# Four transformer blocks on one core: ScalarE's scalings and casts cut into pieces, and another order of the last attention steps

## The chip, the core and the metric

The kernel runs on one core of a Trainium2 chip and is written in Bass: each engine (TensorE, VectorE, ScalarE, GpSimd, and SyncE, which issues the DMAs) has its own program, and they meet in semaphores. The metric is the device time of one execution in microseconds. Before the change it is 1713.87 us, the median of three runs (1713.71 to 1713.95).

## The reference, cut to what matters

`x` has 16 tiles of 128 rows and 512 columns, and so has the context. Each layer adds its output to `x`, scaled with the tanh of a gate.

```python
x = x + tanh(g_xattn[0]) * L0_xattn(layernorm(x), ctx)   # retention
x = x + tanh(g_ffn[0])   * L0_ffn(layernorm(x))          # 8 experts, top 2, and a shared one
x = x + tanh(g_xattn[1]) * L1_xattn(layernorm(x), ctx)   # quantised attention, 16 heads, with cross attention
x = x + tanh(g_ffn[1])   * L1_ffn(layernorm(x))          # dense

# L1_xattn: the normalised input is scaled, clipped and rounded to fp8 for q, k, v; every head is
# normalised; softmax(q k^T) v over its own rows and over the context; the result is scaled by
# proj_smooth, rounded to fp8 and multiplied with wproj (4096 columns in, 512 out)
# L1_ffn:
logits = x @ W_gate.T
routing_weights, _ = top_k(logits, 2)
shared_out = relu(x @ W_up.T) @ W_down.T
expert_out = x @ W_expert
out = shared_out + sum(softmax(routing_weights)) * expert_out
```

## The kernel before

The 16 tiles are 4 chunks (`c`) of 4 tiles (`j`). One execution goes through the retention (`Retention`, `Values`), a block that sorts the rows to experts (`Sorting`), the experts (`Routed`), the shared expert with the quantisation for the next layer (`SharedAndQuantised`, `sh`), the attention, and the dense block (`Dense`, `de`). A barrier of all engines stands between the retention and `Sorting`. Each engine's program is an order written out by hand; an instruction waits for its semaphores, and all behind it on its engine wait too.

**Attention.** It has M = 64 steps: 4 quarters of heads times 16 tiles. `steps` (L2200) calls `step(i, ...)` for every `i` up to 66, since a tile is spread over steps: in step `i` TensorE does `keys_values` and `context_keys_values` of tile `i + 1`, `turn_probs` of `i - 1`, `output` (the projection) of `i - 3`, `turn` (transposes of the normalised heads, L2427) of `i`, `attend` (L2456) of `i - 1`, `scores` of `i` and `queries` of `i + 1`. ScalarE does `exps` of `i - 1` (L2577), `squares_b`, `rows_q`, `squares_a`, `probs_out`, `heads_out`, `values` (L2561), `rows_kv` (`x_kv`, L2522) and `scaled_out` (L2615). VectorE does `maxima` and `probabilities` of `i - 1`, the sum of squares (`sums_b`), the rounding of `y`, `normalise_b` (`t_hn`, L2680), `residual` and `normalise_a`; GpSimd does the power that gives 1 / deviation (`t_rs`) and splits the context.

From a score tile to the next tile's heads the chain runs: `maxima` (VectorE), `exps` (ScalarE), `squares_b` (ScalarE), the sum (VectorE), the power (GpSimd), `normalise_b` (VectorE), `turn` (TensorE).

**The last quantised chunk.** Each of its four slices `k` needs four scalings of 512 columns (`sh.scaled`, L1584; one for each of q, qx, k, v), then a rounding on VectorE in three operations (`sh.rounded`, L1686 to L1692), then a store by SyncE. `scaled` waits until the slice two before it is rounded, because there are two buffers. `LAST_ROWS = (1, 3, 4, 5)` names the steps at whose end ScalarE does all four scalings of a slice; VectorE rounds it at the end of the following step, ahead of that step's `maxima`, and SyncE stores it in between its loads.

**The projection's weight.** At the end of steps 2, 18, 34 and 50 ScalarE casts it (`wproj`, L2538) in two operations of 2048 columns.

**The way into the dense block.** In steps 63 to 66 the dense block's first work stands between the attention's: `de.turn` (transposes of normalised rows, L1863), `de.x_hi` and `de.x_lo` (the split of the transposed rows in a rounded part and a rest, L1870 and L1875), `de.up`, `de.relu`, `de.h_low`, `de.statistics`, `de.normalise`. On VectorE the methods `after_maxima` and `after_residual` place them by step. After that `Dense.tensor` starts with the gate logits of chunk 0, an expert matmul, and `turn_logits` (L1947), and goes on with `turn(3)` (transposes of chunk 3, again L1863).

**The end of the retention.** Each chunk's statistics (`tile_statistics`, L89 and L92) follow its four `x_res` rows. For chunks 0 to 2 GpSimd turns them into 1 / deviation (`row_factors`); for the last chunk ScalarE takes the root and VectorE the reciprocal, after the barrier. `low(2)` (L964), the rest of the split of chunk 2, stands after the barrier too.

## Time and profile before

| | before |
|---|---|
| median of 3 runs | 1713.87 us |
| profiled execution, its own time | 1714.87 us |
| its span | 1713.1 us |
| TensorE busy | 1630.4 us (95%) |
| ScalarE busy | 1102.9 us (64%) |
| VectorE busy | 1081.3 us (63%) |
| GpSimd busy | 480.9 us (28%) |
| DMA, share of 16 engines' span, main queue | 32.0% |
| mean granted TensorE clock | 0.989 |

The profile is one execution with one line for each instruction. In a timeline, equal neighbouring instructions are merged to a row; the brackets at its end give how long the engine was idle before it and what ended that. The durations of neighbouring matmuls and activations overlap, so the distance from start to start is what one costs in a row of them. TensorE's clock is granted at 2.4 GHz (1.00) or half of that.

### The profile page before, as it was taken

The numbers are of one execution on the slowest core, as the hardware profiler recorded it, in microseconds if no ns is written. First come the engines' busy times: TensorE is split into PE (matmuls) and PEld (weight loads), VectorE is DVE, ScalarE is ACT, GpSimd is POOL, SyncE is SP. The second block draws the span as 40 slices with busy tenths as digits, with TensorE's granted clock in tenths as the row PEclk, the third lists the DMA queues.
The fourth block names the chain that finished last, engine by engine and source line by source line (L and its number), as shares of the span: only waits on it lengthen the run. The fifth ranks groups of instructions, "written<-read, shape, count | busy, mean of one in ns | idle before, by whom it ended". The sixth has DMA issues, their size and how long they took to land.

```text
span 1713.1 us, 27138 instructions
## 1 busy us (share of the span) xinstructions
PE 1630.4 (95%) x9136; PEld 1337.7 (78%) x9136; DVE 1081.3 (63%) x2117; ACT 1102.9 (64%) x2974; POOL 480.9 (28%) x511
## 2 busy tenths in 40 slices
PE   6989779999998999999999999999999999998998
PEld 5888656666777778888788888788888788876887
DVE  6158854444876667777777776666666666786322
ACT  3454235543657888888888888878777878873100
POOL 1000122223424233433433433333443333420000
PEclk9999889999999999999999999999999999999999
DMA  6120649885663133364343353121151221100011
GB/s 242 49 80 34 266 138 315 299 287 168 235 237 125 50 127 145 113 265 164 113 152 130 127 225 117 57 86 55 56 233 56 69 79 55 56 25 1 25 37 37
DMA packets 74820, 219.67 MB, mean 128 GB/s; under 512 B 6288, under 2 KB 14480, under 8 KB 68304
## 3 DMA queue, kind: packets, MB, share of 16 engines
q1 hardware_dynamic: 69024, 199.56, 32.0%
q0 software_dynamic: 5680, 18.62, 3.5%
q8 instruction: 66, 1.08, 0.3%
q14 instruction: 50, 0.41, 0.1%
HBM read 157.60 MB, written 60.56 MB: 127 GB/s over the span
## 4 chain that ended last, share of the span: by engine, by line
PE 71%; ACT 5%; DVE 5%; DMA 4%; issue 1%; POOL 1%; another core or an unknown queue 0%; POOLq 0%; ACTq 0%; DVEq 0%
PE bank L2377 9%; PE bank L2378 9%; PE bank L97 7%; PE bank L98 7%; PE bank L99 7%; PE bank L2456 6%; PE bank L2438 6%; PE bank L2469 6%; PE bank L2427 5%; DMA s_rows<-x_rows,t_tok 4%; PE bank L2448 3%; PE bank L1349 3%; PE bank L1369 3%; ACT t_sc L2577 1%; ACT t_y L2615 1%
## 5 line engine op out<-in xcount | busy, mean ns | idle before, releaser
L2680 DVE TENSOR_TENSOR t_hn<-bank,t_rs 128x256 f32<-128x256 f32 (+1 forms) x256 | 130.8, 552 | 137.2 <-POOL t_rs L2342 70.4
L2377 PE MATMUL bank<-t_slot,t_x_q 128*128 128x512 f32 x512 | 205.5, 401 | 0.0
L2339 POOL TENSOR_SCALAR t_ve<-t_ss 128x4 f32<-128x4 f32 (+1 forms) x128 | 25.9, 202 | 628.6 <-DVE t_ss L2676 619.4
L2378 PE MATMUL bank<-t_slot,t_x_q 128*128 128x512 f32 x512 | 200.1, 391 | 0.0
L2577 ACT ACTIVATE t_sc<-bank,t_mx 128x128 f32<-128x128 f32 x512 | 183.9, 455 | 3.5 <-DVE t_mx L2700 3.5
L2342 POOL TENSOR_TENSOR t_rs<-t_ve,t_mhalf 128x4 f32<-128x4 f32 (+1 forms) x128 | 171.0, 1336 | 10.6
L2577 ACT ACTIVATION_READ_ACCUMULATOR t_sc<-bank,t_mx 128x1 f32 x512 | 151.6, 296 | 0.0
L2615 ACT ACTIVATE t_y<-bank,smooth 128x128 bf16<-128x128 f32 x512 | 139.2, 399 | 2.1 <-PE bank L2456 2.1
L2438 PEld LDWEIGHTS bank<-t_hT 128*128 128x128 f32 x1024 | 120.9, 192 | 15.8 <-ACT t_hT L2604 15.0
L2438 PE MATMUL bank<-t_hT 128*128 128x128 f32 x1024 | 131.4, 281 | 1.6 <-ACT t_hT L2604 1.6
L2377 PE MATMUL bank<-t_slot,t_x_kv 128*128 128x256 f32 x512 | 125.3, 283 | 2.1 <-DVE x_res L1647 1.4
L2378 PE MATMUL bank<-t_slot,t_x_kv 128*128 128x256 f32 x512 | 125.6, 283 | 0.0
L2707 DVE RECIPROCAL t_ri<-t_sm 128x4 f32<-128x4 f32 x128 | 22.7, 178 | 162.7 <-ACT t_sc L2577 162.7
L2469 PE MATMUL bank<-t_wp,t_cq 128*128 128x512 f16 x512 | 122.7, 383 | 1.4 <-DVE x_res L2723 1.4
L2456 PE MATMUL bank<-t_pT,t_vv 128*128 128x256 f32 x512 | 122.8, 383 | 0.0
L2377 PEld LDWEIGHTS bank<-t_slot,t_x_q 128*128 128x128 f32 x512 | 96.4, 188 | 18.7
L2378 PEld LDWEIGHTS bank<-t_slot,t_x_q 128*128 128x128 f32 x512 | 96.3, 188 | 18.6
L2427 PE MATMUL bank<-ident,t_hn 128*128 128x128 f32 x768 | 98.5, 275 | 12.1 <-DVE t_hn L2680 12.1
L2427 PEld LDWEIGHTS bank<-ident,t_hn 128*128 128x128 f32 x768 | 88.3, 142 | 27.4 <-DVE t_hn L2680 15.7
L2554 ACT ACTIVATE t_sqk<-bank 128x256 f32<-128x256 f32 x128 | 56.6, 457 | 80.3 <-PE bank L99 77.2
L2377 PEld LDWEIGHTS bank<-t_slot,t_x_kv 128*128 128x128 f32 x512 | 97.7, 191 | 5.1 <-issue 2.7
L2456 PEld LDWEIGHTS bank<-t_pT,t_vv 128*128 128x128 f32 x512 | 93.5, 193 | 10.4
(326 smaller groups left out, 4160.1 us busy)
## 6 DMA issues: line engine op xcount, KB each, us to landing
t_xh<-xq_scratch SPq DMA_DIRECT2D x64, 512.0 KB, 3.6
t_slot<-w_ready SPq DMA_DIRECT2D x16, 2048.0 KB, 8.4
t_cr<-in_ctxT_dram SPq DMA_DIRECT2D x64, 256.0 KB, 2.7
y_rows<-s_y SPq DMA_DIRECT2D x39, 256.0 KB
e_w<-in_w_units_dram SPq DMA_DIRECT2D x8, 1024.0 KB, 11.5
w_rows<-in_w_qkv_dram SPq DMA_DIRECT2D x8, 1024.0 KB, 7.2
w_ready<-w_hi SPq DMA_DIRECT2D x8, 1024.0 KB
w_ready<-w_lo SPq DMA_DIRECT2D x8, 1024.0 KB
```

What stands on the lines that cost most here:

```text
L97: nc.tensor.matmul(out, a_hi, b_hi, start=first, stop=False)
L98: nc.tensor.matmul(out, a_hi, b_lo, start=False, stop=False)
L2342: nc.gpsimd.tensor_tensor(rs[:, lo:hi], ve[:, lo:hi], mhalf[:, lo:hi], ALU.pow).then_inc(rs_in, 1)
L2377: nc.tensor.matmul(out, x_in[:, k, :], w[0][:, k, a:b], start=k == 0, stop=False)
L2378: last = nc.tensor.matmul(out, x_in[:, k, :], w[1][:, k, a:b], start=False, stop=k == KT - 1)
L2427: last = nc.tensor.transpose(b3[out][:, n, :], hn[:, h, :], env.ident[:])
L2438: last = nc.tensor.matmul(b3[4 + part][:, h, :], hT[:, (1 - part) * QH + h, :], hT[:, KH + (1 - part) * QG + h // 2, :], start=True, stop= ...
L2456: last = nc.tensor.matmul(bank[6 + part][:, g * 256:(g + 1) * 256], vv[par][:, (1 - part) * QG + g, :], pT[:, h:h + 2, :], start=True, sto ...
L2469: last = nc.tensor.matmul(bank[5][:], cq[par][:, h, :], wp[:, h, :], start=h == 0, stop=h == KH - 1)
L2577: last = nc.scalar.activation(sc[:, h, :], b3[4 + part][:, n, :], ACT.Exp, bias=mx[:, h:h + 1], accum_out=sm[:, h:h + 1])
L2615: nc.scalar.activation(y[:, part, ramp(h)], b3[6 + part][:, h, :], ACT.Copy, scale=env.smooth8[:, n:n + 1]).then_inc(y_in, 1)
L2680: nc.vector.tensor_tensor(hn[:, lo:hi, :], b3[bk][:, 0:hi - lo, :], rs[:, lo:hi].unsqueeze(2).broadcast_to([P, hi - lo, P]), ALU.mult).the ...
```

## The change

- `sh.scaled` takes the scalings one by one, and `ROW_PIECES` spreads the 16 of the last chunk over steps 1 to 6 (3, 1, 2, 3, 3 and 4 of them). Up to four places in a step take one: between the two squares of `squares_a`, after `heads_out`, after `values`, after `rows_kv`. VectorE's roundings and SyncE's stores stay where they were.
- `wproj` casts in four operations of 1024 columns: after `heads_out`, after `values`, after `rows_kv` and after `scaled_out` of steps 2, 18, 34 and 50.
- The loop of steps ends after step 62 on TensorE, ScalarE and VectorE. What was left stands in `last_steps`, written out for each engine, in another order. In `Dense.tensor` the first expert matmul stands ahead of the gate logits, and the second ahead of `turn_logits`.
- At the retention's end the statistics of three of the last chunk's tiles stand ahead of its last `x_res` row, GpSimd's `row_factors` does that chunk too, and `low(2)` follows ahead of the barrier. Root and reciprocal behind it are gone.

```diff
@@ Values.gpsimd, Values.vector, Sorting.vector
-        for c in range(C - 1):
+        for c in range(C):
             pool.wait_ge(self.final, (c + 1) * 2 * J)
             so.row_factors(pool, c)
...
+                if c == 3 and j == 2:
+                    dve.wait_ge(self.x_in, c * J + j + 1)
+                    for t in range(c * J, c * J + J - 1):
+                        v.bn_stats(env.st[:, t, :], env.x_res[:, t, :]).then_inc(self.final, 1)
             dve.wait_ge(self.x_in, c * J + J)
-            tile_statistics(nc, env, dve, self.final, c * 2 * J, range(c * J, c * J + J))
+            tile_statistics(nc, env, dve, self.final, c * 2 * J, range(c * J, c * J + J), J - 1 if c == C - 1 else 0)
+            if c == C - 1:
+                so.low(dve, 2)
...
-        v.tensor_scalar(self.var[:, 0:J], env.mv[:, last_rows, 1], LN_EPS, None, ALU.add).then_inc(self.var_in, 1)
-        dve.wait_ge(self.roots, 1)
-        v.reciprocal(env.rstd[:, last_rows], self.root[:, 0:J]).then_inc(self.rs_in, 1)
         self.normalise(dve, 3, range(J))
-        self.low(dve, 2)
@@ Dense.expert, Dense.tensor
         if n == 0:
             pe.wait_ge(self.wlo, self.n["expert"])
+        if n == 1:
             pe.wait_ge(self.rows_in, Q * B)
...
+        self.expert(pe, 0, 0)
         self.logits(pe, 0)
-        self.expert(pe, 0, 0)
+        self.expert(pe, 0, 1)
         self.turn_logits(pe, 0)
-        self.expert(pe, 0, 1)
         self.turn(pe, 3, range(2))
@@ attention
+    ROW_PIECES = {1: range(0, 3), 2: range(3, 4), 3: range(4, 6), 4: range(6, 9), 5: range(9, 12), 6: range(12, 16)}
...
+        def last_steps():          # TensorE
+            pe.wait_ge(n_in, M * 4 - 2)
+            de.turn(pe, 0, range(2))
+            turn_probs(M - 2)
+            output(M - 4, M % 2, M * 2 - 2, None)
+            de.turn(pe, 0, range(2, KT))
+            attend(M - 2, M % 2)
+            turn(M - 1)
+            de.turn(pe, 1, range(2))
+            scores(M - 1)
+            de.turn(pe, 1, range(2, KT))
+            de.up(pe, 0, 0)
+            de.up(pe, 0, 1)
+            turn_probs(M - 1)
+            output(M - 3, 1 - M % 2, M * 2, None)
+            attend(M - 1, 1 - M % 2)
+            de.up(pe, 0, 2)
+            output(M - 2, M % 2, M * 2, None)
+            de.up(pe, 0, 3)
+            de.turn(pe, 2, range(2))
+            output(M - 1, 1 - M % 2, M * 2, None)
+            de.turn(pe, 2, range(2, KT))
...
+        def rows_part(i, part):
+            pieces = ROW_PIECES.get(number(i), ())
+            if part < len(pieces):
+                k, v = divmod(pieces[part], 4)
+                sh.scaled(act, C - 1, k, (v,))
+
+        def wproj_part(i, part):
+            if isinstance(i, int) and i % B == 2 and i < M:
+                wproj(i // B, part)
...
             if has(i):
                 heads_out(i)
+            rows_part(i, 1)
+            wproj_part(i, 0)
             if has(i + 1):
                 values(i + 1, 1 - par)
+            rows_part(i, 2)
+            wproj_part(i, 1)
             if has(i + 2):
                 rows_kv(i + 2, par)
+            rows_part(i, 3)
+            wproj_part(i, 2)
             if has(i - 1):
                 scaled_out(i - 1, quarter)
...
-            if number(i) in LAST_ROWS:
-                sh.scaled(act, C - 1, LAST_ROWS.index(i))
-            if isinstance(i, int) and i % B == 2 and i < M:
-                wproj(i // B)
+            wproj_part(i, 3)
+
+        def last_steps():          # ScalarE
+            exps(M - 2)
+            squares_b(M - 1)
+            de.x_hi(act, 0, range(2))
+            probs_out(M - 2)
+            de.x_hi(act, 0, range(2, KT))
+            heads_out(M - 1)
+            de.x_hi(act, 1, range(2))
+            scaled_out(M - 2, None)
+            exps(M - 1)
+            de.relu(act, 0, 0)
+            de.x_hi(act, 1, range(2, KT))
+            de.relu(act, 0, 1)
+            probs_out(M - 1)
+            scaled_out(M - 1, None)
+            de.relu(act, 0, 2)
+            de.high(act, "expert", 0, KT)
+            de.relu(act, 0, 3)
...
+        def last_steps():          # VectorE
+            maxima(M - 2)
+            de.normalise(dve, 1, range(J))
+            probabilities(M - 2)
+            sums_b(M - 1)
+            de.x_lo(dve, 0, range(2))
+            rounded(M - 3, 1 - M % 2, 0)
+            normalise_b(M - 1)
+            de.x_lo(dve, 0, range(2, KT))
+            rounded(M - 3, 1 - M % 2, 1)
+            residual(M - 4, None)
+            de.x_lo(dve, 1, range(2))
+            maxima(M - 1)
+            de.statistics(dve, (10, 11))
+            de.aggregate(dve, 2)
+            probabilities(M - 1)
...
+            rounded(M - 2, M % 2, 1)
+            residual(M - 3, None)
+            de.statistics(dve, (12, 13))
+            de.normalise(dve, 2, range(J))
+            rounded(M - 1, 1 - M % 2, 0)
+            de.h_low(dve, 0, 2)
+            rounded(M - 1, 1 - M % 2, 1)
+            residual(M - 2, None)
+            de.low(dve, "expert", 0, KT)
+            de.h_low(dve, 0, 3)
+            de.x_lo(dve, 2, range(2))
+            residual(M - 1, None)
+            de.x_lo(dve, 2, range(2, KT))
+            de.statistics(dve, (14, 15))
+            de.aggregate(dve, 3)
```

The other lines of the diff drop what the old places held, and pass `end` and `done` to the helpers.

## Rows read from the trace of the kernel before

**Rows 1.** TensorE's waits by line: who was waited for, total us, times, longest us.

```profile
PE bank L2427 <- DVE t_hn L2680: 12.1, 9, 3.0
```

**Rows 2.** TensorE's timeline, `attend`: start us, us, engine, line, operation, idle before.

```profile
538.00 1.89 PE L2456 MATMUL bank<-t_pT,t_vv 128*128 128x256 f32 x8
556.08 3.62 PE L2456 MATMUL bank<-t_pT,t_vv 128*128 128x256 f32 x8
...
576.00 1.89 PE L2456 MATMUL bank<-t_pT,t_vv 128*128 128x256 f32 x8
...
628.20 1.89 PE L2456 MATMUL bank<-t_pT,t_vv 128*128 128x256 f32 x8
...
644.08 1.89 PE L2456 MATMUL bank<-t_pT,t_vv 128*128 128x256 f32 x8
...
818.60 1.89 PE L2456 MATMUL bank<-t_pT,t_vv 128*128 128x256 f32 x8
...
836.79 1.89 PE L2456 MATMUL bank<-t_pT,t_vv 128*128 128x256 f32 x8
```

**Rows 3.** ScalarE's timeline in steps 1 and 18, in the same columns.

```profile
535.17 0.38 ACT L2554 ACTIVATE t_sqk<-bank 128x256 f32<-128x256 f32 x1 [1.20 <-PE bank L99]
...
539.93 0.66 ACT L2561 ACTIVATE t_vv<-bank 128x256 f32<-128x256 f32 x2 [0.88 <-PE bank L2456]
...
543.42 2.98 ACT L1584 ACTIVATE z_y<-z_x3T,qb,qa 128x512 bf16<-128x512 f32 x4
546.24 0.42 ACT L2577 ACTIVATE t_sc<-bank,t_mx 128x128 f32<-128x128 f32 x1
...
820.53 0.66 ACT L2561 ACTIVATE t_vv<-bank 128x256 f32<-128x256 f32 x2 [0.24 <-PE bank L2456]
821.07 1.06 ACT L2522 ACTIVATE t_x_kv<-t_xh 128x1024 fp32r<-128x1024 f16 x1
822.02 2.17 ACT L2615 ACTIVATE t_y<-bank,smooth 128x128 bf16<-128x128 f32 x8
824.01 3.78 ACT L2538 ACTIVATE t_wp<-t_raw 128x2048 f16<-128x2048 f32 x2
827.61 0.43 ACT L2577 ACTIVATE t_sc<-bank,t_mx 128x128 f32<-128x128 f32 x1
```

**Rows 4.** VectorE's timeline in step 6: the last slice's rounding starts.

```profile
631.55 0.68 DVE L1686 TENSOR_SCALAR z_y<-z_y 128x2048 f16<-128x2048 bf16 x1
```

**Rows 5.** ScalarE's timeline, first `exps` after that rounding.

```profile
634.38 0.37 ACT L2577 ACTIVATE t_sc<-bank,t_mx 128x128 f32<-128x128 f32 x1 [0.59 <-DVE t_mx L2700]
```

**Rows 6.** TensorE's timeline on the way into the dense block.

```profile
1531.08 1.03 PE L1863 MATMUL bank<-ident,d_xn 128*128 128x128 f32 x8
...
1580.50 0.95 PE L1947 MATMUL bank<-fold,d_lgT 128*128 128x8 f32 x8
...
1584.18 1.04 PE L1863 MATMUL bank<-ident,d_xn 128*128 128x128 f32 x8
```

**Rows 7.** TensorE's waits from 1531 to 1585 us, by line.

```profile
PE bank L107 <- DVE d_xT_lo L1875: 2.8, 1, 2.8
PE bank L1863 <- DVE d_xT_lo L1875: 2.4, 2, 1.9
PE bank L1863 <- DVE d_xn L1852: 1.5, 1, 1.5
PE bank L2469 <- DVE x_res L2723: 1.4, 1, 1.4
```

**Rows 8.** Stretches: engines' busy us, mean granted clock, DMA share, GB/s.

```profile
1531.00:1563.00 32.00, 28.96 (x166) 22.10 (x163) 20.70 (x46) 19.84 (x57) 3.04 (x4) 1.00 0.00 1
1563.00:1578.00 15.00, 9.29 (x35) 5.84 (x34) 12.86 (x28) 3.12 (x6) 1.20 (x2) 0.77 0.00 1
```

**Rows 9.** VectorE's timeline, first `x_lo` of chunk 3.

```profile
1585.45 1.29 DVE L1875 TENSOR_TENSOR d_xT_lo<-bank,d_xT_hi 128x512 fp32r<-128x512 f32 x2 [0.31 <-ACT d_xT_hi L1870]
```

**Rows 10.** VectorE's timeline, last operation ahead of the retention's barrier.

```profile
189.46 0.38 DVE L92 BATCH_NORM_AGGREGATE mv<-st 128x2 f32<-128x6 f32 x4
```

More of the change, by code:

```diff
@@ L83, in cleared_semaphores, with tile_statistics @@
     nc.all_engine_barrier()
-def tile_statistics(nc, env, dve, stats, count, tiles):
-    for t in tiles:
+def tile_statistics(nc, env, dve, stats, count, tiles, done=0):
+    for t in tiles[done:]:
         nc.vector.bn_stats(env.st[:, t, :], env.x_res[:, t, :]).then_inc(stats, 1)
@@ L871, in __init__ @@
         self.tiles = [sb(f"tiles{i}", [P, 4 + E]) for i in range(3)]
-        self.var, self.root, self.dif, self.e1, self.s1 = (sb(n, [P, B]) for n in ("var", "root", "dif", "e1", "s1"))
+        self.dif, self.e1, self.s1 = (sb(n, [P, B]) for n in ("dif", "e1", "s1"))
         self.graw, self.posf, self.slot, self.row, self.ids = (
@@ L1582, in scaled @@
             act.wait_ge(self.q_in, n - 1)
-        for v in range(4):
+        for v in vs:
             nc.scalar.activation(self.y[n % 2][:, v * CW:(v + 1) * CW], source, ACT.Identity,
@@ L1889, in after_maxima @@
             self.aggregate(dve, 1)
-        if at == -1:
-            self.normalise(dve, 1, range(J))
     def after_residual(self, dve, at):
@@ L1905, in after_residual @@
             self.statistics(dve, (8, 9))
-        if at == -1:
-            self.x_lo(dve, 0, range(2, KT))
-            self.statistics(dve, (10, 11))
-            self.aggregate(dve, 2)
-            self.x_lo(dve, 1, range(2))
-        if at == 0:
-            self.statistics(dve, (12,))
-            self.h_low(dve, 0, 2)
-            self.h_low(dve, 0, 3)
-            self.normalise(dve, 2, range(J))
-        if at == 1:
-            self.statistics(dve, (13,))
-            self.x_lo(dve, 2, range(2))
-        if at == 2:
-            self.statistics(dve, (14,))
     def logits(self, pe, c):
@@ L2100, in vector @@
     def vector(self, dve):
-        self.statistics(dve, (15,))
-        self.aggregate(dve, 3)
-        self.x_lo(dve, 2, range(2, KT))
-        self.low(dve, "expert", 0, KT)
         self.normalise(dve, 3, range(J))
@@ L2202, in side, with steps @@
         return slice((1 - part) * QH, (1 - part) * QH + QH)
-    def steps(eng, step):
+    def steps(eng, step, end=M - 1):
         for i in range(B + FIRST):
@@ L2214, in steps @@
                     step(v * 2 + (first + 1), (FIRST + 1) % 2, quarter)
-            for i in range(first + 2 * loops, first + B):
+            for i in range(first + 2 * loops, min(first + B, end)):
                 step(i, i % 2, None)
@@ L2365, in gpsimd @@
         rstd(0, 0)
-        steps(pool, step)
+        steps(pool, step, M + FIRST)
         de.rstd(pool, 2)
@@ L2513, in tensor @@
         steps(pe, step)
+        last_steps()
         de.tensor(pe)
@@ L2530, in rows_q, with wproj @@
                                  ).then_inc(xq_in, 1)
-        def wproj(quarter):
-            if quarter:
+        def wproj(quarter, part):
+            i, a = divmod(part, 2)
+            if quarter and part == 0:
                 act.wait_ge(pj_ps, quarter * B)
-            act.wait_ge(wraw_in, quarter * 16 + 16)
+            if part == 0:
+                act.wait_ge(wraw_in, quarter * 16 + 16)
             raw = slots32[homes[quarter][SPARE]]
-            for i in range(2):
-                nc.scalar.activation(wp[:, 4 * i:4 * i + 4, :], raw[:, i], ACT.Copy).then_inc(wp_in, 1)
+            last = nc.scalar.activation(wp[:, 4 * i + 2 * a:4 * i + 2 * a + 2, :], raw[:, i, 2 * a:2 * a + 2, :], ACT.Copy)
+            if a:
+                last.then_inc(wp_in, 1)
+        def rows_part(i, part):
[6 more added lines that the diff above has]
+                wproj(i // B, part)
         def squares_a(m):
@@ L2734, in step @@
                 probabilities(i - 1)
-            if number(i) == M:
-                de.x_lo(dve, 1, range(2, KT))
-                de.h_low(dve, 0, 0)
             if has(i) and later(i, 1):
@@ L2741, in step @@
                 rounded(i - 2, par, 0)
-            if number(i) == M - 1:
-                de.x_lo(dve, 0, range(2))
-            if number(i) == M:
-                de.h_low(dve, 0, 1)
             if number(i) == M - 3:
@@ L2773, in step @@
                 sh.rounded(dve, C - 1, LAST_ROWS.index(i - 1))
+        def last_steps():
[14 more added lines that the diff above has]
+            probabilities(M - 1)
+            de.h_low(dve, 0, 0)
+            de.x_lo(dve, 1, range(2, KT))
+            rounded(M - 2, M % 2, 0)
+            de.h_low(dve, 0, 1)
+            rounded(M - 2, M % 2, 1)
[13 more added lines that the diff above has]
+            de.aggregate(dve, 3)
         sh.normalise(dve, C - 1)
```

48 lines of the change are left out of this document (7 added, 41 removed).

## The prediction

> **What bounds the kernel now.** I read the page first: TensorE is busy 95% of the span, and two thirds of the span (504 to 1570 us) are 64 attention steps. Then the waits of TensorE by line: the largest sum inside the attention is the transposes of the normalised heads, which stood 12.1 us for VectorE's `t_hn` [rows 1]. Then TensorE's timeline, one row per step (the row of `attend`): it shows where steps are longer than usual. A usual step is 15.88 us, from 628.20 to 644.08, with no idle time: there TensorE alone sets the pace. Between attend 0 (538.00) and attend 5 (628.20) stand 90.20 us. Four usual steps and the step into attend 1, which has no `output` yet (15.87 less the 1.73 from the start of `output` to the next group, so 14.14), make 77.6 us: 12.6 us are lost [rows 2]. From attend 17 to attend 18 stand 18.19 us, so 2.3 are lost, and the same after the casts of quarters 2 and 3: 7.0 us in three places. The rest of the middle has nothing to give. Last I read the way from attention to the dense block: from 1531.08, the first `de.turn`, to 1584.18, the first `turn` of chunk 3, stand 53.10 us [rows 6], with 8.1 us of waits in four rows [rows 7] and a mean granted clock of 0.77 in 1563 to 1578 [rows 8].
>
> **Why pieces of ScalarE work cost time.** ScalarE goes from `values` through `rows_kv` and `scaled_out` to the next `exps` without a pause; its last pause before that is 0.24 us ahead of `values`, or 0.88 in a step in which TensorE has been held. Two casts of 2048 columns moved `exps` from 824.01 to 827.61, by 3.60 us; four scalings of 512 columns moved it from 543.42 to 546.24, by 2.82 [rows 3]. `exps` leads to the squares, VectorE's sum, GpSimd's power and VectorE's `t_hn`. The delays of 3.60 and 2.82 lost 2.3 and 1.5 us a step (the latter from attend 2 at 576.00 to attend 5 at 628.20, three steps of 17.40 [rows 2]), so this chain has 1.3 us of slack: a step loses the delay of its `exps` less 1.3. That rule carries the first sum.
>
> **The last quantised chunk.** Its 16 scalings ran as four blocks; they become 3, 1, 2, 3, 3 and 4 pieces in steps 1 to 6. One piece takes 2.82/4 = 0.71 us. The first of a step goes between the two squares, where ScalarE stood 1.2 us for TensorE [rows 3]: free. The second goes ahead of `values` and fills the 0.24 or 0.88 us. The others count in full.
> - Step 1: one piece counts, delay 0.71, and the power chain has 1.73 us less slack in the step without `output`, so it loses 0.71 - (1.3 - 1.73) = 1.1. Now it loses 3.9 there, with the wait of 3.0 [rows 1], and TensorE falls to half speed: attend 1 took 3.62 us where 1.89 is usual [rows 2]. A stall of 1.1 should not bring that on; the saved 2 us lie in step 2's present loss of 4.1.
> - Step 2: one free piece and all four parts of the weight cast, three of them in full (below): delay 2.9, loss 1.6.
> - Step 3: nothing. Step 4: 2 x 0.71 - 0.24 = 1.2. VectorE's rounding of a finished slice stands ahead of the maxima: from its start (631.55) to `exps` (634.38) stand 2.83 us [rows 4, 5]; by that way too the delay is 1.2. Step 5 gives 1.3. Both are at the edge of the slack: loss 0 to 0.1 each.
> - Step 6 is the new stall. Its last piece stands behind `rows_kv`, and the rounding of that slice, in VectorE's program ahead of the maxima, waits for it. From `values` on, with a piece ahead of it (0.47 late): pair of casts 0.54, piece 0.71, `x_kv` 0.95, piece 0.9 to its end makes 3.6; rounding to `exps` 2.83. So `exps` starts 6.4 us after the usual start of `values` instead of 3.48 [rows 3]: delay 2.9, loss 1.6. SyncE's store of the slice waits for the rounding too, 2.1 us later than now, and behind it in SyncE's queue stand the KV weights, `t_cr` and `t_xh` of tile 9. By my sum `t_xh` comes 0.1 us before it is wanted; I price it at 0, with 0.5 as the other end.
> Together 1.1 + 1.6 + 0 + 0.1 + 1.6 = 4.4 us lost against 12.6: **8.2 us gained** (5 to 10).
>
> **The weight casts of quarters 1 to 3.** Two of 2048 columns become four of 1024. `x_kv`, also 1024 columns, holds ScalarE from 821.07 to 822.02, 0.95 us [rows 3]. All four stand between `heads_out` and `exps` of the same step, so the delay is 4 x 0.95 - 0.24 = 3.56 against 3.60: nothing is gained, 0.1 us in all. The waits that they put ahead of `values`, `x_kv` and `y` (0.7, 1.7 and 2.6 us) are hidden: TensorE wants `x_kv` 3.7 us after it is now ready. The page Perfetto Trace Analysis of the Trainium skill (§ Optimizing Scalar/DVE Operations) says that breaking up instructions helps where an unsaturated ScalarE causes bubbles elsewhere. It would have these three stalls shrink; rows 3 show no pause for the pieces to fall into. That is the second rival.
>
> **The last steps.** On TensorE the same items stand in a new order. Their durations without stalls, from start to start of the 24 groups in the timeline from 1531.08 to 1584.18 [rows 6]: a pair of turns 0.87 (six), a turn of probabilities 0.87 (two), `output` 1.73 (four), `attend` 1.73 (two), head turns 1.31, scores 1.80, `up` 2.72 (four), experts 2.72 (two), gate logits 1.82, their turn 0.81. Sum 39.4. So 13.7 us are lost now: 8.1 in the waits, 15 x (1 - 0.77) = 3.4 from half speed [rows 7, 8], the rest in a small wait and in restarts.
> I walked the new order with these durations and those of ScalarE and VectorE. Squares now come ahead of the copies of `xT`, the sum follows the probabilities at once, and x_lo(0) is done at 1534.6, as TensorE wants it: the wait of 1.9 goes. Scores 63 follow the head turns with only one pair of turns between, but need all copies of the heads (3.05 us after the head turns start, as in usual steps): a new wait of 0.9. `turn_probs` 63 comes 1.4 us after its probabilities. Both last `output`s find their rounded input, because `up` 2 and 3 stand between them. `normalise` 2 is done at 1555 for a turn at 1560, x_lo(2) at 1564.9, while the expert matmul (now ahead of the logits) covers until 1566. So turn 3 starts at 1531.1 + 39.4 + 0.9 = 1571.4 instead of 1584.2: 12.8 us.
> What is late next: the turn of the logits moved behind the second expert, so VectorE's gate weights and its x_lo(3) come closer to the turns that need them. x_lo(3) starts 4.95 us after the turn of the logits (1580.50 to 1585.45 [rows 6, 9]), its first slice is done 0.65 later; TensorE has 0.81 + 0.87 + 2.72 = 4.4 us of work. A new wait of about 1.0. Left: **11.8 us gained** (7 to 12.8).
>
> **The front.** Statistics of three tiles go under the last `output`, the root goes to GpSimd, and `low(2)` moves ahead of the barrier. VectorE reached the barrier at 189.84 [rows 10]; it is to be done with the statistics 1.8 us earlier and then does four `low`s of 0.62, so it is there 0.65 later. `normalise` 3 still starts where it did. GpSimd's constants, for which the turn of the logits waits, start 0.65 later too; about 0.4 of it is made up behind, where TensorE now waits for x_lo(3) and no longer will: **0.2 us lost** (0.4 gained to 0.7 lost). The block behind (routing on VectorE) is unchanged.
>
> **Sum.** 8.2 + 0.1 + 11.8 - 0.2 = 19.9 us. The profiled execution took 1714.87 us, 1.0 above the median of the runs, and its span is 1713.1; I take the gain off both alike: 1695.0 for a profiled execution and 1713.87 - 19.9 = **1694.0 us** for the median. The forecast's own range, from the bounds of its parts, is 1691 to 1698.
>
> **Rivals.**
> - The pieces work everywhere, also in quarters 1 to 3: the three losses of 2.3 us go. For it: the edit is the same as in steps 1 to 5, where it helps. Against it: all four parts stand in one step without a pause. 1694.0 - 6.9 = 1687.1. 8%.
> - The last steps give half: a wait that my walk gets wrong by a microsecond (the scores, x_lo 3, the last `output`) brings the half-speed clock back, as two waits of 1.5 and 1.4 us do now. 1694.0 + 5.9 = 1700. 13%.
> - The first edit does not do what it says: the pieces only move the same ScalarE work and the delays of `exps` stay, with late slices behind SyncE's queue. 1713.9 - 11.7 = 1702. 6%.
> - Slower: TensorE stays at 1.2 GHz through the whole transition. Half speed was granted right when it had idled at 551 and again after 1563, and the new order has short waits of 0.9 and 1.0. At half speed the 39.4 us of work take 39.4 more, so 1694.0 + 39.4 = 1733.4; it makes the kernel slower from 20 us of work at half speed on. Against it: the granted clock was 1.00 from 1531 to 1563, past a wait of 1.9 [rows 7, 8]. 2%.
> The forecast has 69%, 2% is left for what I don't see. A difference of 0.2% (3.4 us) is about what a measurement of this kernel can tell from none. Range: the forecast, and to 1701 for the second rival, which holds 82%: 1689 to 1701. Faster 0.95, same 0.02, slower 0.03.
>
> **What would show it.** Right: attend 1 to 5 at full speed, steps 4 and 5 near 15.9 us, a stall of 1.6 in the head turns of step 7, where none is now; steps 18, 34 and 50 still with 2.3; in the last steps one wait of 0.9 ahead of scores and one of 1.0 at turn 3. Wrong: steps 18, 34 and 50 at 15.9 (rival one), a granted clock below 1 after 1530 (rivals two and four), `exps` as late in steps 2 to 5 as now (rival three), or a wait for `t_xh` near tile 9.

## The result, and the profile after

The changed kernel takes 1693.2 us, the median of four runs (1690.65 to 1694.76), beside 1713.91 us for the kernel before, now of four runs: a ratio of 0.9872, 95% interval 0.9853 to 0.9892. The two medians lie 20.7 us apart. Two later series gave 0.9888 (0.9865 to 0.9911) and 0.9897 (0.9874 to 0.9920). As gains the three ratios are 21.9, 19.2 and 17.6 us. In the later series single executions of the kernel before took 1707 to 1719 us, so each ratio is known to 0.2% and no better. 1694.0 was forecast.

The profiled execution took 1690.65 us (span 1688.9). The spans of the two profiles differ by 24.2 us, more than the medians. Part of it isn't the change's: at attend 0 the second profile is already 4.17 us ahead, and nearly all of that comes from the routed and the shared experts, whose code is the same (last section).

The page's first lines, busy time and the granted clock in 40 slices of the span:

```profile
PE 1625.2 (96%) x9136; PEld 1337.6 (79%) x9136; DVE 1081.9 (64%) x2115; ACT 1104.6 (65%) x2981; POOL 482.0 (29%) x513
...
PEclk9999979999999999999999999999999999999999
```

TensorE's timeline of the changed kernel, the row of `attend` (L2435), with the head turns (L2406) ahead of two of them; columns as in [rows 2]:

```profile
533.83 1.89 PE L2435 MATMUL bank<-t_pT,t_vv 128*128 128x256 f32 x8
549.14 1.89 PE L2435 MATMUL bank<-t_pT,t_vv 128*128 128x256 f32 x8
566.60 1.89 PE L2435 MATMUL bank<-t_pT,t_vv 128*128 128x256 f32 x8
...
630.50 1.25 PE L2406 MATMUL bank<-ident,t_hn 128*128 128x128 f32 x8 [1.04 <-DVE t_hn L2686]
631.59 1.89 PE L2435 MATMUL bank<-t_pT,t_vv 128*128 128x256 f32 x8
...
647.59 1.89 PE L2435 MATMUL bank<-t_pT,t_vv 128*128 128x256 f32 x8
...
806.26 1.89 PE L2435 MATMUL bank<-t_pT,t_vv 128*128 128x256 f32 x8
...
823.22 1.25 PE L2406 MATMUL bank<-ident,t_hn 128*128 128x128 f32 x8 [1.31 <-DVE t_hn L2686]
824.31 1.89 PE L2435 MATMUL bank<-t_pT,t_vv 128*128 128x256 f32 x8
```

These answer [rows 2]. Each `attend` takes 1.89 us: the one of 3.62 is gone. From attend 0 to 7 stand 113.76 us, where 121.93 stood before: **8.17 us gained**. The step into attend 18 takes 18.04 us where 18.19 stood, so the stall of quarter 1 is still there, with its wait of 1.31 for `t_hn`; those of quarters 2 and 3 are alike (18.04 and 18.05). From attend 7 to 61: **0.3 us gained**. TensorE's waits for `t_hn` over the whole profile (total, times, longest), beside [rows 1]:

```profile
PE bank L2406 <- DVE t_hn L2686: 7.7, 7, 1.3
```

ScalarE's timeline in steps 6 and 18, which answers [rows 3 and 5]:

```profile
618.77 0.83 ACT L1582 ACTIVATE z_y<-z_x3T,qb,qa 128x512 bf16<-128x512 f32 x1
619.47 2.19 ACT L2613 ACTIVATE t_y<-bank,smooth 128x128 bf16<-128x128 f32 x8
622.47 0.37 ACT L2575 ACTIVATE t_sc<-bank,t_mx 128x128 f32<-128x128 f32 x1 [0.81 <-DVE t_mx L2706]
...
807.83 1.06 ACT L2522 ACTIVATE t_wp<-t_raw 128x1024 f16<-128x1024 f32 x1
...
814.15 1.15 ACT L2522 ACTIVATE t_wp<-t_raw 128x1024 f16<-128x1024 f32 x1
815.10 0.46 ACT L2575 ACTIVATE t_sc<-bank,t_mx 128x128 f32<-128x128 f32 x1
```

In step 18 the four parts stand between 807.83 and 815.10, where ScalarE has no pause left, and `exps` starts 8.84 us after attend 17 (806.26). Before it was 9.01; in a usual step it is 5.42. The delay is still 3.42. In step 6 `exps` waits for the maxima behind the last slice's rounding.

The way into the dense block, in TensorE's timeline (L1861 `de.turn`, L2417 scores, L1928 `turn_logits`), then two stretches of it with TensorE's busy time, granted clock, DMA share and GB/s; these answer [rows 6, 7 and 8]:

```profile
1518.42 1.03 PE L1861 MATMUL bank<-ident,d_xn 128*128 128x128 f32 x8
...
1527.55 2.05 PE L2417 MATMUL bank<-t_hT 128*128 128x128 f32 x16 [0.70 <-ACT t_hT L2602]
...
1558.15 0.95 PE L1928 MATMUL bank<-fold,d_lgT 128*128 128x8 f32 x8
1558.96 1.15 PE L1861 MATMUL bank<-ident,d_xn 128*128 128x128 f32 x8
1563.52 1.16 PE L1861 MATMUL bank<-ident,d_xn 128*128 128x128 f32 x8 [0.68 <-DVE d_xT_lo L1873]
```

```profile
1518.00:1550.00 32.00, 31.30 (x184) 1.00 0.00 1
1550.00:1565.00 15.00, 14.32 (x80) 1.00 0.01 1
```

From the first `de.turn` to turn 3 stand 40.54 us instead of 53.10. The clock is 1.00 in both stretches, and only the two forecast waits are left, 0.70 and 0.68. From attend 61 to the last `turn_logits` 90.70 us instead of 102.24: **11.54 us gained**. With the 4.17 ahead of attend 0 that makes 24.18.

### The profile page after: what moved, and what is told of

It reads as the page before. It is cut to its first block, busy times and chain, and to the rows that moved or that the text cites. A ratio compares the mean times of both kernels' runs of the same rounds, so it can differ in the third digit from the quotient of the medians.

```text
span 1688.9 us, 27156 instructions
## 1 busy us (share of the span) xinstructions
PE 1625.2 (96%) x9136; PEld 1337.6 (79%) x9136; DVE 1081.9 (64%) x2115; ACT 1104.6 (65%) x2981; POOL 482.0 (29%) x513
## 4 chain that ended last, share of the span: by engine, by line
PE 76%; ACT 4%; DVE 3%; DMA 3%; POOL 1%; issue 1%; ACTq 0%; POOLq 0%; DVEq 0%
PE bank L2356 10%; PE bank L2357 10%; PE bank L97 7%; PE bank L98 7%; PE bank L99 7%; PE bank L2417 7%; PE bank L2435 6%; PE bank L2448 6%; PE bank L2406 5%; PE bank L1347 3%; PE bank L1367 3%; PE bank L2427 3%; DMA s_rows<-x_rows,t_tok 2%; PE bank L1327 1%; ACT t_sc L2575 1%
## 5 line engine op out<-in xcount | busy, mean ns | idle before, releaser
L2417 PEld LDWEIGHTS bank<-t_hT 128*128 128x128 f32 x1024 | 120.2, 191 | 16.8 <-ACT t_hT L2602 16.2
L2417 PE MATMUL bank<-t_hT 128*128 128x128 f32 x1024 | 131.0, 281 | 2.3 <-ACT t_hT L2602 2.3
L2435 PE MATMUL bank<-t_pT,t_vv 128*128 128x256 f32 x512 | 121.1, 379 | 0.0
L2406 PEld LDWEIGHTS bank<-ident,t_hn 128*128 128x128 f32 x768 | 87.6, 141 | 22.7 <-DVE t_hn L2686 10.7
L2406 PE MATMUL bank<-ident,t_hn 128*128 128x128 f32 x768 | 97.3, 274 | 7.7 <-DVE t_hn L2686 7.7
L97 PE MATMUL bank<-t_slot,t_c_hi 128*128 128x512 f32 x256 | 100.4, 392 | 0.0
```

The costliest lines, as they stand in the source:

```text
L97: nc.tensor.matmul(out, a_hi, b_hi, start=first, stop=False)
L2406: last = nc.tensor.transpose(b3[out][:, n, :], hn[:, h, :], env.ident[:])
L2417: last = nc.tensor.matmul(b3[4 + part][:, h, :], hT[:, (1 - part) * QH + h, :], hT[:, KH + (1 - part) * QG + h // 2, :], start=True, stop= ...
L2435: last = nc.tensor.matmul(bank[6 + part][:, g * 256:(g + 1) * 256], vv[par][:, (1 - part) * QG + g, :], pT[:, h:h + 2, :], start=True, sto ...
```

## The experiments

**Each part alone.** Four kernels, each the kernel before with one part of the change. The interval after each ratio to the kernel before is the 95% one.

*Only the pieces of the last chunk:*

```diff
+    ROW_PIECES = {1: range(0, 3), 2: range(3, 4), 3: range(4, 6), 4: range(6, 9), 5: range(9, 12), 6: range(12, 16)}
...
-            if number(i) in LAST_ROWS:
-                sh.scaled(act, C - 1, LAST_ROWS.index(i))
             if isinstance(i, int) and i % B == 2 and i < M:
                 wproj(i // B)
```

> The kernel before with the last quantised chunk in pieces, and nothing else (the weight casts stay two of 2048 columns at the end of steps 2, 18, 34, 50). Slack theory: a step loses the delay of its exps beyond 1.3 us. Step 1 loses 1.1, step 2 has a delay of 3.6 and loses 2.3, step 6 loses 1.6, against 12.6 now: 7.5 us gained between attend 0 and attend 7, nothing elsewhere, about 1706.4. If the pieces only moved the same work (the third rival of the prediction), 0 to 2 us would be gained and exps in steps 2 to 5 would be as late as before.

1704.66 us, ratio 0.9962 (0.9948 to 0.9977), 6.5 us. Its `attend` rows:

```profile
533.88 1.89 PE L2457 MATMUL bank<-t_pT,t_vv 128*128 128x256 f32 x8
549.18 1.89 PE L2457 MATMUL bank<-t_pT,t_vv 128*128 128x256 f32 x8
567.38 1.89 PE L2457 MATMUL bank<-t_pT,t_vv 128*128 128x256 f32 x8
...
648.25 1.89 PE L2457 MATMUL bank<-t_pT,t_vv 128*128 128x256 f32 x8
```

Attend 0 to 7: 114.37 us, 7.56 less than before (7.5 expected). The steps lose 1.16, 2.32 and 1.39 us in the three places where 1.1, 2.3 and 1.6 were expected, and steps 3 to 5 nothing. The rival that the pieces only move the same work falls.

*Only the parts of the weight cast:*

```diff
...
+            wproj_part(i, 0)
             if has(i + 1):
                 values(i + 1, 1 - par)
+            wproj_part(i, 1)
             if has(i + 2):
                 rows_kv(i + 2, par)
+            wproj_part(i, 2)
             if has(i - 1):
                 scaled_out(i - 1, quarter)
+            wproj_part(i, 3)
...
-            if isinstance(i, int) and i % B == 2 and i < M:
-                wproj(i // B)
```

> The kernel before with the weight casts as four operations of 1024 columns between ScalarE's other work of steps 2, 18, 34 and 50, and nothing else. Slack theory: exps is delayed by 3.56 instead of 3.60 us in each of these steps, so the steps into attend 18, 34 and 50 lose 2.2 to 2.3 us as before; 0.1 to 0.6 us in all, 1713.3 to 1713.8. Breaking-up theory (first rival): the three stalls and that of step 2 go, 7 to 9 us gained, about 1705.

1711.23 us, ratio 0.9999 (0.9988 to 1.0009). The steps into attend 18, 34 and 50 take 18.03, 18.02 and 18.02 us, 0.17 less than before each. ScalarE in that step:

```profile
815.04 1.07 ACT L2539 ACTIVATE t_wp<-t_raw 128x1024 f16<-128x1024 f32 x1
815.98 0.67 ACT L2568 ACTIVATE t_vv<-bank 128x256 f32<-128x256 f32 x2
816.51 1.09 ACT L2539 ACTIVATE t_wp<-t_raw 128x1024 f16<-128x1024 f32 x1
817.46 1.09 ACT L2522 ACTIVATE t_x_kv<-t_xh 128x1024 fp32r<-128x1024 f16 x1
818.41 1.08 ACT L2539 ACTIVATE t_wp<-t_raw 128x1024 f16<-128x1024 f32 x1
```

No row has a pause ahead of it: beyond the 0.24 us ahead of `values` the parts found no idle time to fall into. Smaller pieces in the same stretch of work gained nothing that can be timed. The first rival falls here. Attend 0 to 7 takes 120.29 us in this profile, 1.64 less than before, and nearly all of that is the clock's: half speed held for 3.4 us near attend 1 instead of 6.8.

*Only the last steps* (`last_steps` on three engines and the order of `Dense.tensor`, as in the diff of the change):

```diff
+        self.expert(pe, 0, 0)
         self.logits(pe, 0)
-        self.expert(pe, 0, 0)
+        self.expert(pe, 0, 1)
         self.turn_logits(pe, 0)
-        self.expert(pe, 0, 1)
```

> The kernel before with only the new order of the last steps and of the first items of the dense block (expert matmul ahead of the gate logits, the second ahead of turn_logits). Order theory: 11.5 to 11.8 us gained between attend 61 and the first turn of chunk 3, granted clock 1.00 from the first turn of the dense block on, waits of 0.7 to 0.9 ahead of scores 63 and 0.7 to 1.0 ahead of turn 3; about 1702.2. If the gain in this place needed the earlier edits too, or the half-speed clock came back: 5.9 us, about 1708.

1700.73 us, ratio 0.9930 (0.9916 to 0.9943), 12.0 us. Attend 61 to the last `turn_logits` takes 90.69 us. The two stretches of [rows 8] in this kernel (engines' busy time, clock, DMA share, GB/s):

```profile
1531.00:1563.00 32.00, 31.30 (x185) 24.77 (x184) 28.69 (x60) 21.63 (x59) 3.35 (x4) 1.00 0.00 1
1563.00:1578.00 15.00, 14.32 (x78) 11.90 (x77) 10.79 (x30) 4.00 (x8) 1.20 (x2) 1.00 0.01 1
```

TensorE is busy 14.32 of 15 us at full clock, where 9.29 at 0.77 stood. This part needs none of the others.

*Only the front:*

```diff
-        for c in range(C - 1):
+        for c in range(C):
...
+            if c == C - 1:
+                so.low(dve, 2)
```

> The kernel before with only the edit at the end of the retention (statistics of three tiles earlier, root on GpSimd, low of chunk 2 ahead of the barrier). From the comparison of the two kernels: between 0.2 us lost and 0.1 us gained, 1713.8 to 1714.1. If the edit is instead what changed the routed experts' waits for gathered rows (12.2 us before, 7.4 after) and the shared stage, it gains 4 us: about 1710.

1713.31 us, ratio 1.0009 (0.9996 to 1.0022). TensorE's first row behind the barrier in the kernel before, in this one, and in the changed kernel's third profile, and then the engines' busy time and the clock (0.72) of this kernel there:

```profile
190.94 0.47 PE L107 MATMUL bank<-b_xThi,r_wg 128*128 128x512 f32 x1 [1.24 <-PEq L83]
```

```profile
191.04 0.55 PE L107 MATMUL bank<-b_xThi,r_wg 128*128 128x512 f32 x1 [1.83 <-PEq L83]
```

```profile
190.84 0.47 PE L107 MATMUL bank<-b_xThi,r_wg 128*128 128x512 f32 x1 [1.83 <-PEq L83]
```

```profile
191.00:197.00 6.00, 5.96 (x31) 5.24 (x32) 3.73 (x20) 2.18 (x5) 2.59 (x20) 0.72 0.88 251
```

The barrier is waited for 1.83 us where it was 1.24, so it opens 0.59 us later (0.65 forecast). What that costs depends on the clock. From the first gate logits (`b_xThi`) to the first scan matmul stand 20.10 to 20.12 us in the four kernels without this part. With it they are 19.96 to 19.97 in six profiles and 20.59 to 20.61 in four, and in those four, this one among them, the clock is at half speed for a few us just behind the barrier. With this part the stretch is 0.15 us shorter or 0.5 longer. None of the four profiles without it has half speed there; that is too few to say whether the later barrier brings it on, and no run settles it. The waits of the routed experts (10.1 us in this kernel, 9.5 to 12.2 in the four without the edit, 7.4 to 12.1 in the ten with it) are not its doing.

Together the four ratios make 1.00%, 17 us. In the profiles the sum of the places is 7.56 + 0.42 + 11.55 us, less 0.5 or plus 0.15: 19.0 to 19.7.

**The changed kernel again, and three kernels made from it.**

> The changed kernel once more, in one series with the next three. If its parts add up: the sum of the four parts alone (ratios 0.9962, 0.9999, 0.9930, 1.0009) gives 0.9900 and some 17 us below the kernel before of the same series; the prediction's sum gives 0.9884 (19.9 us). If the parts help each other it would be the 0.9872 of the first comparison or less.

1693.02 us, ratio 0.9888 (0.9865 to 0.9911), between the two sums; the interval holds both. Attend 0 to 7 takes 113.91, 7 to 61 863.19 and 61 to the last `turn_logits` 90.64 us, like the first profile. There is no sign that the parts help each other.

*The gate logits first again* (the last diff above undone):

> The changed kernel with the gate logits of chunk 0 again ahead of the first expert matmul and turn_logits ahead of the second. The walk of the order: x_lo(2) comes later than the logits want it, a wait of 1.4 to 1.8 us ahead of the logits, and the wait of 0.7 at turn 3 goes: 0.7 to 1.1 us slower than the changed kernel (ratio to it about 1.0005). If the expert-first order were what holds the clock up: a granted clock below 1 in the 15 us behind it and 3 to 6 us slower.

1693.54 us, ratio 0.9889 (0.9867 to 0.9911); the times can't tell it from the changed kernel. The trace can: TensorE's waits from 1520 to 1570 us are

```profile
PE bank L107 <- DVE d_xT_lo L1873: 1.7, 1, 1.7
PE bank L2417 <- ACT t_hT L2602: 0.7, 1, 0.7
```

The logits now wait 1.7 us for x_lo(2), the wait at turn 3 is gone, and the stretch from attend 61 to the last `turn_logits` takes 91.60 us, 0.96 more. The clock stays at 1.00 in this profile, so the expert-first order is worth 1 us and is not what holds the clock.

*Doses.* Copies that no one reads, of 0.95 us each, in two places of otherwise usual steps (the loop over the steps is shortened, so that these steps stand outside it):

```diff
+    KV_AGAIN = {44: 1, 46: 2, 48: 3}
+    Q_AGAIN = {38: 2, 40: 3, 42: 4}
...
+            again(KV_AGAIN.get(number(m) - 2, 0), xh[par][:, :, 2:4, :].rearrange("p k v s -> p v k s"))
             nc.scalar.activation(x_kv[:], xh[par][:, :, 2:4, :].rearrange("p k v s -> p v k s"), ACT.Copy
```

> The changed kernel with copies of 1024 columns that nobody reads added on ScalarE: one, two and three between values and x_kv in steps 44, 46 and 48, and two, three and four between the second squares_b and x_q in steps 38, 40 and 42. Each costs 0.95 us. Slack theory (a step loses its exps's delay less 1.3, after a pause of 0.24 ahead of values that the copies here stand behind and so cannot use: delays 0.95, 1.90, 2.85): losses of 0, 0.6 and 1.55 us ahead of attend 44, 46 and 48; the copies ahead of x_q fall in the pause of 1.57 between the two squares_a and in that of 1.52 ahead of heads_out and lose 0, 0 and 0 to 0.2. If any ScalarE work costs the same wherever it stands: losses grow alike in both places, 0.6 per copy or more.

The usual pauses of ScalarE behind `exps`, in the changed kernel (between the two squares, and ahead of `heads_out`):

```profile
836.47 0.39 ACT L2552 ACTIVATE t_sqk<-bank 128x256 f32<-128x256 f32 x1 [1.57 <-PE bank L99]
...
839.51 0.56 ACT L2596 ACTIVATE t_hT<-bank,par 128x256 f32<-128x256 f32 x1 [1.52 <-PE bank L2406]
```

ScalarE in step 48 of the kernel with the doses, and TensorE's `attend` 47 and 48:

```profile
1292.09 0.66 ACT L2568 ACTIVATE t_vv<-bank 128x256 f32<-128x256 f32 x2 [0.24 <-PE bank L2437]
1292.63 2.95 ACT L2505 ACTIVATE z_y<-t_xh 128x1024 bf16<-128x1024 f16 x3
1295.47 1.06 ACT L2513 ACTIVATE t_x_kv<-t_xh 128x1024 fp32r<-128x1024 f16 x1
1296.42 2.17 ACT L2622 ACTIVATE t_y<-bank,smooth 128x128 bf16<-128x128 f32 x8
1298.42 0.43 ACT L2584 ACTIVATE t_sc<-bank,t_mx 128x128 f32<-128x128 f32 x1
```

```profile
1290.16 1.89 PE L2437 MATMUL bank<-t_pT,t_vv 128*128 128x256 f32 x8
1307.61 1.89 PE L2437 MATMUL bank<-t_pT,t_vv 128*128 128x256 f32 x8
```

| copies | where | delay of `exps`, us | lost, us | expected |
|---|---|---|---|---|
| 1 | ahead of x_kv | 0.95 | 0 | 0 |
| 2 | ahead of x_kv | 1.89 | 0.63 | 0.6 |
| 3 | ahead of x_kv | 2.84 | 1.57 | 1.55 |
| 2, 3 | ahead of x_q | 0 | 0 | 0 |
| 4 | ahead of x_q | 0 | 0.30 | 0 to 0.2 |

Three copies ahead of `exps` cost 1.57 us, and three behind it nothing; the fourth there is more than the two pauses hold (3.80 us of copies, 3.09 of pauses). The delays are those from `attend` to `exps` (8.26 us from 1290.16 to 1298.42) less the usual 5.42. The slack is 1.26 and 1.27 us in the doses that lose (1.89 - 0.63, 2.84 - 1.57). This is the rule of the prediction measured by itself. The kernel took 1695.28 us (two runs), ratio 0.9900 (0.9866 to 0.9933); its losses are too small to be read from the times.

*Two parts moved on*, in the weight cast of each quarter:

```diff
-            if isinstance(i, int) and i % B == 2 and i < M:
+            if isinstance(i, int) and i % B == 2 + part // 2 and i < M:
                 wproj(i // B, part)
...
                 if part:
                     rows_part(m - 1, 0)
+                    wproj_part(m - 1, 2)
+                    wproj_part(m - 1, 3)
...
-            wproj_part(i, 2)
             if has(i - 1):
                 scaled_out(i - 1, quarter)
-            wproj_part(i, 3)
```

In this kernel and in the three edits that follow, the loop over the usual steps also starts one step later (`FIRST, LOOPS = 4, 3`), so that step 3 of a quarter stands outside it.

> The changed kernel with two of the four parts of each weight cast moved on: parts 2 and 3 stand between the two squares_a of steps 3, 19, 35 and 51, where ScalarE pauses 1.57 us in a usual step. Slack theory: exps of steps 19, 35 and 51 is delayed by 2 x 0.95 - 0.24 = 1.66 instead of 3.56, so the steps into attend 18, 34 and 50 lose 0.4 instead of 2.2; step 2 loses 0.4 to 0.9 instead of 1.6: 6 us gained, a ratio of 0.9965 to the changed kernel. If the number of pieces and not their place decides: these steps stay at 18.04 us and nothing is gained.

1691.72 us, ratio 0.9883 (0.9860 to 0.9906), which the times can't tell from the changed kernel's 0.9888. The steps into attend 18, 34 and 50 take 17.10 to 17.11 us: 0.94 gained in each place, not 1.8. `exps` came as early as expected. A new wait took the rest; the row of `output` 16:

```profile
819.87 1.90 PE L2448 MATMUL bank<-t_wp,t_cq 128*128 128x512 f16 x8 [1.05 <-ACT t_wp L2522]
```

The first tile of a quarter wants the new weight in that very step, 1.05 us before its last part was cast. Step 2 went the same way: it loses 1.34 us where 0.4 to 0.9 was expected, with a wait of 1.29 us for the weight. So 2.6 us are gained from attend 7 to 61 and none ahead of it, where 6 was expected. That place decides stands; who reads the weight, and when, was missing from the expectation.

**All of it in pauses.** The changed kernel once more, as the measure, and then two kernels that put the parts where the trace shows ScalarE idle and early enough for `output`.

> The changed kernel once more, as the measure for the next two in the same series: 0.988 to 0.989 of the kernel before.

1695.05 us, ratio 0.9897 (0.9874 to 0.9920).

The next edit is to this kernel:

```diff
-            if isinstance(i, int) and i % B == 2 and i < M:
+            if isinstance(i, int) and i % B == (3 if part else 2) and i < M:
                 wproj(i // B, part)
...
                 squares_b(i)
+            for part in range(1, 4):
+                wproj_part(i, part)
             if has(i + 1):
                 rows_q(i + 1, 1 - par)
...
-            wproj_part(i, 1)
...
-            wproj_part(i, 2)
...
-            wproj_part(i, 3)
```

> The changed kernel with part 0 of each weight cast behind heads_out of steps 2, 18, 34 and 50, and parts 1 to 3 behind squares_b of steps 3, 19, 35 and 51, so that they end ahead of output 16, 32 and 48 (with two parts between the squares output waited 1.05 us for them). Slack theory: exps is delayed by 0.95 - 0.24 = 0.71, under the slack of 1.3; the parts end 0.1 us before output wants them: the steps into attend 18, 34 and 50 take 15.9 to 16.1 instead of 18.04, step 2 loses 0 to 0.5 instead of 1.6: 7.5 us gained, ratio to the changed kernel 0.9956. If output waits for them all the same: 0.5 to 1 us lost in each place.

1686.79 us, ratio 0.9846 (0.9821 to 0.9871), clear of the changed kernel's in the same series. The same row as above, and ScalarE ahead of it:

```profile
821.52 1.90 PE L2448 MATMUL bank<-t_wp,t_cq 128*128 128x512 f16 x8
```

```profile
817.39 1.23 ACT L2566 ACTIVATE t_hn<-bank 128x512 f32<-128x512 f32 x2
818.35 3.11 ACT L2522 ACTIVATE t_wp<-t_raw 128x1024 f16<-128x1024 f32 x3
```

The parts end at 821.46, just ahead of `output` at 821.52, which waits for nothing. No step from 8 to 61 is over 15.95 us: attend 7 to 61 takes 857.40 us, 6.4 less than in the profile of the changed kernel of this series (863.78). The steps into attend 2 and 3 lose 0.12 and 0.63 where 1.58 and 0 stood. From attend 0 to 61 that makes 7.4 us in the trace, 7.5 expected.

And now the scalings, from the kernel casts_ahead on:

```diff
+    ROW_PIECES = {1: ((0, 1), ()), 2: ((2, 3), ()), 3: ((), (4, 5)), 4: ((6, 7), (8, 9)), 5: ((10, 11), (12, 13)),
+                  6: ((14, 15), ())}
...
+            rows_part(m, 1)
             act.wait_ge(t_ps, m * 3 + 1)
             nc.scalar.activation(hT[:, KH:KH + QG, :], b3[4][:, 0:2, :], ACT.Identity, scale=env.col("head_wb", 2),
```

> The kernel casts_ahead with the 16 scalings of the last chunk in ScalarE's pauses: pieces 0 and 1 between the squares_a of step 1, 2 and 3 there in step 2, 4 and 5 ahead of heads_out's wait in step 3, 6 to 9 in both places of step 4, 10 to 13 in both of step 5, 14 and 15 between the squares of step 6. Slack theory: no exps is late by them; step 1 loses 0.4 (no output in it) instead of 1.2, step 6 nothing instead of 1.4 to 1.6: 2.2 us beyond casts_ahead, about 9.7 us below the changed kernel, ratio to it 0.9943, some 1683. If the pieces that share a pause delay the second square, probs_out or heads_out enough to hold attend or the scores: 0.3 to 1 us lost in each of steps 3 to 5 and less gained than that.

1683.02 us, ratio 0.9835 (0.9811 to 0.9859). Attend 0 to 7 takes 111.39 us. Step 1 loses 0.46 (0.4 expected), step 6 nothing, but the step into attend 3 loses 1.3, at the scores:

```profile
568.90 2.05 PE L2418 MATMUL bank<-t_hT 128*128 128x128 f32 x16 [1.17 <-ACT t_hT L2603]
```

Three parts of the cast and two scalings are 4.3 us in a step whose pauses hold 1.57 + 1.52. The scores then wait for the copies of the heads. The last kernel empties that step:

```diff
-    ROW_PIECES = {1: ((0, 1), ()), 2: ((2, 3), ()), 3: ((), (4, 5)), 4: ((6, 7), (8, 9)), 5: ((10, 11), (12, 13)),
-                  6: ((14, 15), ())}
+    ROW_PIECES = {1: ((0, 1), (), ()), 2: ((2, 3), (), ()), 4: ((4, 5), (6, 7), (8,)),
+                  5: ((9, 10), (11, 12), (13,)), 6: ((14, 15), (), ())}
...
                 heads_out(i)
+            rows_part(i, 2)
```

> The kernel in_pauses with no scaling in step 3, where three parts of the weight cast already fill ScalarE's pauses (scores 3 waited 1.17 us there for the copies of the heads, the step took 17.20 us): pieces 4 to 8 in step 4 (two between the squares, two ahead of heads_out, one behind it), 9 to 13 in step 5 in the same places. Pause theory: a piece behind heads_out delays exps by 0.71 - 0.24 = 0.47, under the slack, so steps 4 and 5 stay near 15.9 us and the step into attend 3 takes 15.9 to 16.1: 1.1 to 1.3 us less from attend 0 to attend 7 (111.39 becomes 110.2), about 1682, ratio to the kernel before 0.983. If five pieces in a step are too many for its pauses, the steps into attend 4 and 5 take 16.2 to 16.5 and half of it or all is lost again.

1683.33 us, ratio 0.9839 (0.9814 to 0.9864). The step into attend 3 takes 15.88 us, and attend 0 to 7 takes 110.43. The steps into attend 4 and 5 take 15.96 and 16.13 (15.88 before), so 0.96 us is gained in the trace where 1.1 to 1.3 was expected. The times of two series don't resolve 1 us. Both kernels are faster than the one before and than the changed one. The interval of in_pauses ends at 0.9859, and that of the changed kernel in the same series starts at 0.9874; one_step_free ran in a series of its own, where it was compared with the kernel before alone. From attend 0 to 61 that kernel's profile needs 977.97 us, in_pauses 968.43 and one_step_free 967.32.

## Why the prediction was right

**The slack rule held.** A step loses the delay of its `exps` less 1.3 us: that carried the first sum. The doses measured 1.27 by itself, and step 18 of the changed kernel gives 1.26 again (delay 3.42, loss 2.16). For steps 1 to 6, forecast and measured losses are 1.1 and 1.17, 1.6 and 1.58, 0 and 0, 0 to 0.1 and 0.08, 0 to 0.1 and 0, 1.6 and 1.40. The gain is 8.2 us as forecast. One thing in it is not ScalarE's. `attend` 1 at half speed [rows 2] comes in some executions and not in others: with the same wait of 3.00 us ahead of it, the kernel with only the front shows full clock there and needs 119.84 us from attend 0 to 7 instead of 121.93. At full clock steps 1 and 2 are 2.4 us shorter there (0.3 of it goes again in step 4, at the turn of the probabilities). So some 2 of the 8.2 us depend on the execution of the kernel before, and the forecast took them as always there.

**Step 6 came by the way that was named**, as a stall in the head turns of step 7. The step lost 1.40 instead of 1.6: `exps` was 2.74 late (622.47 less attend 5 at 614.31, less the usual 5.42), not 2.9. The late store behind it cost 0.12 us in the step into attend 7 (0.10 to 0.55 in the eight profiles of kernels with this step), not by `t_xh`, as the prediction feared, but by `t_cr`, which it had named without a price: SyncE loads the context tile behind the store, GpSimd waits for it, the power for the next heads stands behind that, and VectorE's `t_hn` and maxima behind the power, so `exps` is late again.

```profile
632.74 1.50 POOL L2309 TENSOR_SCALAR t_c_hi<-t_cr 128x512 fp32r<-128x512 f32 x1 [3.01 <-DMA t_cr<-in_ctxT_dram]
```

In the two kernels with no stall in step 6 the step into attend 7 takes 15.88 again. `t_xh` was as close as the prediction had it: in one profile (moved_casts) ScalarE waited 0.16 us for it, at no cost.

**The weight casts:** 0.1 us forecast for the three, 0.3 to 0.5 measured. The delay is 3.42, not 3.56, because the first part hides 0.38 us and not 0.24: in casts_ahead, where it stands alone, `exps` is only 0.57 late. The extra 0.14 is about what two ScalarE operations in a row overlap (a part takes 1.07 us, and the next row starts 0.94 after it); that an operation behind a pause loses this overlap is my reading, and no run tests it. By the Trainium skill (Perfetto Trace Analysis, Optimizing Scalar/DVE Operations), breaking up instructions may help where ScalarE is unsaturated and causes bubbles. The traces agree with it in part: the pieces gained in the steps where they reached a pause, and next to nothing where they stood in one block of work. The prediction calls the rival that goes with this its second; in its list it is the first.

**The last steps:** 11.8 forecast, 11.5 measured. What the walk said of the waits was met: the wait of 1.9 went, the new ones were 0.70 (0.9 forecast) and 0.68 (1.0), and turn 3 starts 12.6 us earlier, counted from the first `de.turn` (12.8). For the second wait the prediction's own terms give 4.95 + 0.65 - 4.4 = 1.2, which it rounded to 1.0. It is shorter because x_lo(3) starts 4.54 us after `turn_logits`, not the 4.95 of [rows 6 and 9]:

```profile
1562.69 1.28 DVE L1873 TENSOR_TENSOR d_xT_lo<-bank,d_xT_hi 128x512 fp32r<-128x512 f32 x2
```

How much of it is the clock can be told from four kernels with the old order. They need 100.55, 102.24, 103.20 and 103.40 us from attend 61 to the last `turn_logits`, with half speed in 3.4, 6.8, 10.2 and 10.2 us of it. The nine profiles with the whole new order need 90.6 to 90.7, with no half speed. Rivals two and four, which needed it, fall. A line through the four gives some 99 us at full clock, an estimate: 8 to 9 us are the order's and the rest, 1 to 4, the clock's, for which the prediction had 3.4.

**The front:** 0.2 us lost was forecast, within 0.4 gained and 0.7 lost; it is 0.15 gained or 0.5 lost. The barrier opens later by the amount forecast (0.59 for 0.65), but whether the part gains or loses goes with the clock behind it, which was no term of the forecast.

**The sum** of the three places in the first pair of profiles is 8.17 + 0.3 + 11.54 = 20.0 us, where 8.2 + 0.1 + 11.8 = 20.1 was forecast. That the first median came within 1 us of 1694.0 is partly luck: three series of the same kernel give gains of 17.6 to 21.9, and some 4 to 5 us of the 20.0 are half speed in the profile of the kernel before (2 near attend 1 and about 3 in the last steps, an estimate from the lines above), which the other profiles without that part of the change show in other amounts. The range of 1691 to 1698 that the prediction draws from the bounds of its parts doesn't follow from them: they add up to 1691 to 1702.

## What to carry to other kernels

When an engine is free a third of the time, ask where: the same work cost nothing behind `exps`, in pauses of 1.57 and 1.52 us, and cost its whole length less 1.3 us ahead of it. Cutting work into pieces only makes it movable; each piece then has to be put into a pause, before its reader wants it, and no step may get more than its pauses hold. Measure the slack of the chain once, with work that no one reads, and then place by that number.
